# Attention on one Trainium2 core: the reciprocal of the softmax sums taken ahead of the first shift, and its transposes put between the third and fourth turn

## The chip, the core and the metric

The kernel runs on one core of a Trainium2 chip. The metric is the device time of one execution in microseconds (us). The kernel before takes 1241.21 us, the median of three runs from 1240.40 to 1241.44.

## The reference

The input x is one image of 128 x 128 positions with 64 channels. Four layers run one after the other, each as x = x + layer(group_norm(x)). The change touches the first one alone, attention along the rows of the image:

```
x = layernorm(pair)                                  # over 64 channels
q = (x @ Wq) * scale;  k = x @ Wk;  v = x @ Wv       # 4 heads of 32
bias = x @ Wb;  gate = sigmoid(x @ Wg + bg)
attn = softmax(q.k + bias, over the keys)            # per row i and head: 128 x 128
out = gate * (attn @ v)
x1 = pair + out @ Wo + bo
```

There are 128 rows, and in each row four heads of 128 x 128 scores, all in fp32. The other three layers are a windowed attention with a convolution, a graph diffusion in eight Runge-Kutta steps, and a row and column equivariant layer with 15 weights.

## The kernel before

Four rows make a group, so there are 32 groups (ROWS = 4, GROUPS = 32). The loop of the attention stage (`layer0_attention`, from L565) has 34 steps: in step g the engines work on three groups at once, as a pipeline. Group g is "own" (scores, shift, subtraction, exponential), group g - 1 is "past" (its probabilities are turned, weighted with v, and summed), and group g - 2 is "older" (its sums are inverted, and the result is gated, projected and added to x). Each engine has a list of its own, written out by hand in the order in which it runs, and waits at semaphores for the others; nothing reorders it.

The path of one group through the engines:

- TensorE makes the scores (`scores`, L789) in the PSUM banks called quad, one bank for each head.
- VectorE shifts them (`shift_head`, L703): for each of four rows of a head one instruction adds the bias, negates, writes the result to the SBUF tile `prob`, and keeps the least of each line in `least`. There are 16 for a group.
- GpSimd subtracts `least`, head by head (L639), and ScalarE takes the exponential in place, head by head (L667).
- One step later TensorE turns the probabilities (`turn`, L797), four transposes for each of four rows. The turned rows share two PSUM banks, so row 2 waits for ScalarE's copy (`keep_turn`, L662) of row 0, and row 3 for that of row 1. Then `weigh` (L803) makes attn @ v, and `add_up` (L811) the sums over keys, as products with a matrix that picks a head. VectorE copies the sums to SBUF (L759).
- One step later still, TensorE transposes the sums (L829, semaphore sums_turned) right behind its scores. VectorE takes their reciprocal (L722, rtotal_ready), 128 x 16 numbers. GpSimd spreads each of them over 32 columns (L645, rwide_ready). TensorE transposes that back, four transposes of 128 x 128 (L840, r_made), into the bank `total_bank`. VectorE multiplies it with 1 + tanh of the gate (L732) and with attn @ v (L738, gated_ready), TensorE projects with Wo (L852), and VectorE adds the result to x (L744, x1_ready).

TensorE's list in a steady step is thus: scores; transpose of the older sums; turns of rows 0 and 1; turns 2 and 3, each behind its copy; the four reciprocal transposes; q and k of the next group (L773, which waits until two heads of this group are shifted); gate and v of this group (L779, L782, which wait until all four copies of the turns are made, as they write to the same two banks); output projection (L852); weigh; add_up.

VectorE's list is: shift head 0; reciprocal; shift heads 1 and 2; factor and gated; shift head 3; x1; v with its bias (L751); copy of the sums; two statistics of x1 for the next layer (L762, L763). GpSimd's is: subtract head 0; spread; subtract heads 1 to 3; two copies of x1 to the other half of the partitions (L654). ScalarE's is: four copies of turns; exponential of head 0; q and k of the next group (L671, L673); exponential of head 1; tanh of the gate (L692); exponentials of heads 2 and 3.

The first two steps have no older group, the last two no own one, and the last one no past one. Step 31 has an own group, but no next one to project.

Of the kernel before, what the change touches and what calls it, by code (L numbers as in the profile page):

```python
# [16 lines left out]
HEADS, HD = 4, 32  # L17
ROWS = 4
# [546 lines left out]
def layer0_attention(nc, m, args):  # L565
# [19 lines left out]
    rtotal = m.take(ROWS * HEADS)  # L585
    rwide = m.take(CH)
# [4 lines left out]
    scores_made, shifted, lowered, exps_done = S("scores_made"), S("shifted"), S("lowered"), S("exps_done")  # L591
    turned, kept = S("turned"), S("kept")
    av_made, sums_made, sums_kept, sums_turned = S("av_made"), S("sums_made"), S("sums_kept"), S("sums_turned")
    rtotal_ready, rwide_ready, r_made, factor_ready, gated_ready = S("rtotal_ready"), S("rwide_ready"), S("r_made"), S("factor_ready"), S("gated_ready")
# [11 lines left out]
    def of_head(t, h):  # L606

        return t.rearrange("p (r h x) -> p h r x", r=ROWS, h=HEADS)[:, h, :, :]
# [11 lines left out]
    with nc.Block() as block:  # L620

        @block.sync
        def _(sp):
            sp.dma_start(wo, args["L0_conv_Wo"]).then_inc(wo_ready, 16)

        @block.gpsimd
        def _(pool):
            step = m.chain(pool, "pool")
            step(pool.memset(pick, 0.0))
            for h in range(HEADS):  # L630
                step(pool.memset(pick[:, h, h:h + 1], 1.0))
            pool.sem_inc(pick_ready, 1)  # L632
            for g in range(STEPS0):
                b = g % 2
                for h in range(HEADS):
                    if g < GROUPS:
                        pool.wait_ge(shifted, HEADS * g + h + 1)
                        scored = of_head(prob[b], h)
                        pool.tensor_tensor(scored, scored, of_head(least[b], h).broadcast_to([128, ROWS, L]),  # L639
                                           ALU.subtract).then_inc(lowered, 1)  # L640
                    if h == 0 and g >= 2:
                        pool.wait_ge(rtotal_ready, g - 1)
                        if g > 2:
                            pool.wait_ge(r_made, g - 2)
                        pool.tensor_copy(rwide.rearrange("p (x d) -> p x d", d=HD),  # L645
                                         rtotal.unsqueeze(2).broadcast_to([128, ROWS * HEADS, HD])).then_inc(rwide_ready, 1)
                if g >= 2:
                    pool.wait_ge(rwide_ready, g - 1)
                    if g < GROUPS:
                        pool.wait_ge(lowered, HEADS * (g + 1))  # L650
                    pool.wait_ge(x1_ready, g - 1)
                    for e in range(2):
                        there, here = slice(e * C, (e + 1) * C), slice((1 - e) * C, (2 - e) * C)
                        step(pool.tensor_copy(m.pairs(HALF * (g - 2), HALF, m.x1s)[there], m.pairs(HALF * (g - 2), HALF)[here]))  # L654
# [43 lines left out]
        @block.vector  # L698
        def _(dve):

            def shift_head(g, b, h):
                for r in range(ROWS):
                    last = dve.tensor_tensor_reduce(prob[b][:, at(r, h)], m.quad[:, h, row(r)], m.bias[:, row(h)],  # L703
                                                    -1.0, BIG, ALU.add, ALU.min, least[b][:, at(r, h, 1)])
                last.then_inc(shifted, 1)

            dve.wait_ge(wo_ready, 16)
            dve.tensor_scalar(wo, wo, 0.5, None, ALU.mult).then_inc(S("wo_halved"), 1)
            dve.wait_ge(m.sem("bias_laid"), 16 * 64)
            for g in range(STEPS0):  # L710
                b = g % 2
                own, past, older = g < GROUPS, 1 <= g <= GROUPS, g >= 2
                if own:
                    dve.wait_ge(scores_made, g + 1)
                    if g >= 2:
                        dve.wait_ge(turned, 4 * (g - 1))
                    shift_head(g, b, 0)
                if older:
                    dve.wait_ge(sums_turned, g - 1)
                    if g >= 3:  # L720
                        dve.wait_ge(rwide_ready, g - 2)
                    dve.reciprocal(rtotal.rearrange("p (r h) -> p r h", r=ROWS),  # L722
                                   total_bank[:, 0:128].rearrange("p (r x) -> p r x", r=ROWS)[:, :, 0:HEADS]).then_inc(rtotal_ready, 1)
                if own:
                    shift_head(g, b, 1)
                    shift_head(g, b, 2)
                if older:
                    dve.wait_ge(r_made, g - 1)
                    dve.wait_ge(th_ready, g - 1)
                    if g >= 3:  # L730
                        dve.wait_ge(gated_ready, g - 2)
                    dve.scalar_tensor_tensor(out=factor, in0=th[b], scalar=1.0, in1=total_bank[:, :],  # L732
                                             op0=ALU.add, op1=ALU.mult).then_inc(factor_ready, 1)
                    dve.wait_ge(factor_ready, g - 1)
                    dve.wait_ge(av_made, g - 1)
                    if g >= 3:
                        dve.wait_ge(out_made, g - 2)
                    dve.tensor_tensor(gated, av_bank[:, :], factor, ALU.mult).then_inc(gated_ready, 1)  # L738
                if own:
                    shift_head(g, b, 3)  # L740
                if older:
                    dve.wait_ge(out_made, g - 1)
                    inner = m.pairs(HALF * (g - 2), HALF)
                    dve.scalar_tensor_tensor(out=inner, in0=total_bank[:, 0:PAIR].rearrange("p (i c) -> p i c", i=2),  # L744
                                             scalar=m.bo[:, :], in1=inner, op0=ALU.add, op1=ALU.add).then_inc(x1_ready, 1)
                if own:
                    dve.wait_ge(th_ready, g + 1)
                    if g >= 2:
                        dve.wait_ge(av_made, g - 1)
                    for half, bank in enumerate((turn_a, turn_b)):  # L750
                        last = dve.tensor_tensor(v[b][:, half * 256:(half + 1) * 256].rearrange("p (i c) -> p i c", i=2),  # L751
                                                 bank[:, 256:512].rearrange("p (i c) -> p i c", i=2),
                                                 m.v_bias[:, :].unsqueeze(1).broadcast_to([128, 2, 128]), ALU.add)
                    last.then_inc(v_ready, 1)
                if past:
                    dve.wait_ge(sums_made, g)
                    if g >= 2:
                        dve.wait_ge(sums_turned, g - 1)
                    dve.tensor_copy(sums, total_bank[:, 0:128]).then_inc(sums_kept, 1)  # L759
                if older:  # L760
                    dve.wait_ge(x1_ready, g - 1)
                    dve.bn_stats(m.stats[:, (g - 2) * 6:(g - 1) * 6], inner)  # L762
                    dve.tensor_reduce(m.cell_parts[:, (g - 2) * KVW:(g - 1) * KVW],  # L763
                                      inner.rearrange("p r (k w) -> p k r w", k=KVW), AX.XY, ALU.add)

        @block.tensor
        def _(pe):
# [25 lines left out]
            def turn(g, r):  # L793
                for h in range(HEADS):
                    if r == 0:
                        pe.wait_ge(exps_done, HEADS * g + h + 1)
                    last = pe.transpose(m.bank[r % 2][:, row(h)], prob[g % 2][:, at(r, h)], ident)  # L797
                last.then_inc(turned, 1)
# [19 lines left out]
            for g in range(STEPS0):  # L818
                b = g % 2
                own, past, older = g < GROUPS, 1 <= g <= GROUPS, g >= 2  # L820
# [9 lines left out]
                if past:  # L830
                    pe.wait_ge(v_ready, g)
                    turn(g - 1, 0)
                    turn(g - 1, 1)
                    for r in range(2, ROWS):
                        pe.wait_ge(kept, 4 * (g - 1) + r - 1)
                        turn(g - 1, r)
                if older:
                    pe.wait_ge(rwide_ready, g - 1)
                    for r in range(ROWS):
                        last = pe.transpose(total_bank[:, row(r)], rwide[:, row(r)], ident)  # L840
                    last.then_inc(r_made, 1)
                if g + 1 < GROUPS:
                    pe.wait_ge(shifted, HEADS * g + 2)
                    project_qk(g + 1)
# [947 lines left out]
```

## Time and profile before

| what | value |
|---|---|
| median of 3 runs | 1241.21 us (1240.40 to 1241.44) |
| profiled execution | 1242.17 us, its span 1240.4 us |
| busy share of the span | PE 89%, PEld 62%, DVE 59%, ACT 46%, POOL 26% |
| mean granted TensorE clock | 0.939 of full speed |
| attention stage (L620 to L863) | about 156 to 459 us of the span |
| one steady step of it | 8.97 us |

PE is TensorE's matmul row and PEld its row of weight loads, which run ahead of the matmuls and beside them; every transpose here is a load and a matmul. DVE is VectorE, ACT ScalarE, POOL GpSimd. The span is the time from the first to the last instruction; the execution takes 1.8 us more than that. In a timeline row the first number is the start, the second the duration of the row's instructions together, the bracket at the end the idle time ahead of them on their engine and what ended it. The names after the operation are tiles: "quad", "bank" and "duo" are PSUM ("duo" holds total_bank and av_bank), "nat" holds `prob` and the turned rows, "arena" is the tile space in SBUF that holds q, k, v, rtotal, rwide and the rest.

### The profile page before, as it was taken

What the parts mean: (1) busy time and instruction counts of PE and PEld (TensorE: products, weight loads), DVE (VectorE), ACT (ScalarE), POOL (GpSimd) and SP (SyncE); (2) the same over time, 40 slices, a digit from 0 to 9 for tenths busy, and PEclk for the clock granted to TensorE, in tenths of its full rate; (3) what the DMA queues carried; (4) which work ended last, traced back from release to release, by engine and by line L of the source; (5) the groups of instructions that cost most, each with busy time, mean ns of one, the idle gap of its engine ahead of it and who ended that gap; (6) DMA issues with size and microseconds to landing.
All of it is one profiled execution on the core that took longest, in us unless ns stands there. A gap on an engine that the chain in (4) does not pass through costs nothing. (4 is left out here: it accounts for less than half of the span.)

```text
span 1240.4 us, 25484 instructions
## 1 busy us (share of the span) xinstructions
PE 1098.8 (89%) x9447; PEld 770.5 (62%) x9447; DVE 728.6 (59%) x3560; ACT 569.3 (46%) x1161; POOL 325.6 (26%) x466
## 2 busy tenths in 40 slices
PE   3677289999999969994999999999999999999688
PEld 2422067777777743443777677677777767776476
DVE  2521057787877752224566766766676677667235
ACT  1299556767676631002444444444444444443200
POOL 0100046656565631000112212221221122122111
PEclk9987679999999988995999999999999999999869
DMA  8000000000000000000000000000000000000002
GB/s 156 1 0 4 4 4 3 2 3 2 3 2 3 3 1 1 1 0 9 2 1 1 1 2 1 1 2 1 1 2 1 1 1 1 1 1 1 1 29 112
DMA packets 11487, 11.35 MB, mean 9 GB/s; under 512 B 4324, under 2 KB 9188, under 8 KB 11364
## 3 DMA queue, kind: packets, MB, share of 16 engines
q1 hardware_dynamic: 9266, 9.08, 2.9%
q8 instruction: 75, 1.23, 0.4%
q10 hardware_dynamic: 2098, 0.65, 0.3%
q14 instruction: 48, 0.39, 0.1%
HBM read 5.14 MB, written 4.23 MB: 8 GB/s over the span
## 5 line engine op out<-in xcount | busy, mean ns | idle before, releaser
L1460 PE MATMUL quad<-theta,nat 128*128 128x512 f32 x512 | 240.7, 593 | 0.0
L639 POOL TENSOR_TENSOR nat<-nat,arena 128x512 f32<-128x512 f32 x128 | 132.9, 1050 | 111.4 <-DVE arena L703 111.4
L1259 POOL TENSOR_TENSOR nat<-nat,const 128x512 f32<-128x512 f32 x32 | 40.6, 1268 | 439.4 <-DVE nat L1398 439.4
L1468 PEld LDWEIGHTS quad<-flat 128*128 128x128 f32 x768 | 104.6, 190 | 46.5 <-ACT flat L1290 25.1
L1468 PE MATMUL quad<-flat 128*128 128x128 f32 x768 | 123.8, 284 | 2.8 <-ACT flat L1290 1.7
L1460 PEld LDWEIGHTS quad<-theta,nat 128*128 128x128 f32 x512 | 87.5, 191 | 61.7 <-issue 61.7
L703 DVE CUSTOM_DVE_ANT_0 nat<-quad,arena 128x128 f32<-128x128 f32 x512 | 113.2, 283 | 9.7 <-PE quad L789 9.7
L1290 ACT ACTIVATE flat<-quad 128x256 f32<-128x256 f32 x192 | 73.4, 382 | 70.4 <-PE quad L1468 56.6
L662 ACT ACTIVATE nat<-bank 128x512 f32<-128x512 f32 x128 | 69.5, 595 | 57.2 <-PE bank L797 57.2
L1367 DVE SCALAR_TENSOR_TENSOR flat<-nat,c,duo 128x128 f32<-128x128 f32 x64 | 22.0, 345 | 102.0 <-PE duo L1477 102.0
L667 ACT ACTIVATE nat<-nat 128x512 f32<-128x512 f32 x128 | 77.2, 633 | 5.6 <-POOL nat L639 5.5
L797 PE MATMUL bank<-const,nat 128*128 128x128 f32 x512 | 70.0, 280 | 8.0 <-ACT nat L662 8.0
L1456 PE MATMUL bank<-nat 128*128 128x128 f32 x512 | 68.8, 278 | 0.3 <-DVE nat L1444 0.3
L797 PEld LDWEIGHTS bank<-const,nat 128*128 128x128 f32 x512 | 56.0, 141 | 18.1 <-ACT nat L662 15.6
L1456 PEld LDWEIGHTS bank<-nat 128*128 128x128 f32 x512 | 63.1, 194 | 0.9 <-DVE nat L1444 0.7
L1348 ACT ACTIVATE nat<-bank 128x512 f32<-128x512 f32 x32 | 19.1, 597 | 87.3 <-PE bank L1565 87.3
L1383 DVE MAX8 arena<-nat 128x8 f32<-128x128 f32 x128 | 27.9, 281 | 44.4 <-ACT nat L1327 44.4
L773 PE MATMUL quad<-flat,w 64*128 64x256 f32 x256 | 38.2, 419 | 15.0 <-POOLq L632 13.0
L1415 DVE CUSTOM_DVE_ANT_0 nat<-nat,duo 128x128 f32<-128x128 f32 x128 | 29.2, 284 | 37.1 <-PE duo L1576 37.1
L703 DVE DVE_READ_ACCUMULATOR2_ANT arena<- 128x1 f32 x512 | 42.6, 83 | 0.0
L671 ACT ACTIVATE arena<-quad,qkg_bias 128x512 f32<-128x512 f32 x32 | 22.0, 687 | 41.5 <-PE quad L773 41.5
L512 PE MATMUL quad<-arena,const 128*128 128x512 f32 x32 | 22.7, 798 | 20.5 <-ACT arena L475 20.5
(384 smaller groups left out, 2316.2 us busy)
## 6 DMA issues: line engine op xcount, KB each, us to landing
out<-nat SPq DMA_DIRECT2D x16, 256.0 KB, 2.0
arena<-flat SPq DMA_DIRECT2D x64, 4.0 KB
const<-in_constants ACTq DMA_DIRECT2D x1, 400.5 KB, 3.2
arena<-in_L_conv_Ws SPq DMA_DIRECT2D x1, 240.0 KB
flat<-arena SPq DMA_DIRECT2D x3, 32.0 KB, 4.3
nat<-in_x SPq DMA_DIRECT2D x4, 0.2 KB, 13.0
arena<-in_L_conv_Wq ACTq DMA_DIRECT2D x1, 32.0 KB, 7.8
arena<-in_L_conv_Wk ACTq DMA_DIRECT2D x1, 32.0 KB, 7.7
```

The costliest lines, as they stand in the source:

```text
L639: pool.tensor_tensor(scored, scored, of_head(least[b], h).broadcast_to([128, ROWS, L]), ALU.subtract).then_inc(lowered, 1)
L662: act.activation(pT[r], m.bank[r % 2][:, :], ACT.Copy).then_inc(kept, 1)
L667: act.activation(t, t, ACT.Exp, scale=-1.0).then_inc(exps_done, 1)
L703: last = dve.tensor_tensor_reduce(prob[b][:, at(r, h)], m.quad[:, h, row(r)], m.bias[:, row(h)], -1.0, BIG, ALU.add, ALU.min, least[b][:, ...
L773: last = pe.matmul(bank, m.w0[part, w * 128:(w + 1) * 128], m.z[part, cols], start=True, stop=True)
L797: last = pe.transpose(m.bank[r % 2][:, row(h)], prob[g % 2][:, at(r, h)], ident)
L1259: pool.tensor_tensor(quarters(rem), quarters(rem), ident.unsqueeze(1).broadcast_to([128, ROWS, 128]), ALU.add).then_inc(diag_added, 1)
L1290: act.activation(kept, m.quad[:, HALF * half:HALF * (half + 1), place * C:(place + 2) * C], ACT.Copy).then_inc(z_ready[half], 1)
L1415: last = dve.tensor_tensor_reduce(cor[:, col(n)], rem[:, col(n)], B[2][:, col(n)], 1.0, 0.0, ALU.add, ALU.add, deg[:, n:n + 1])
L1456: last = pe.matmul(B[0][:, col(n)], source[:, col(n)], source[:, col(n)], start=True, stop=True)
L1460: return pe.matmul(m.quad[:, n, :], vT[:, col(n)], m.theta[:, part, :], start=(part == 0), stop=False, skip_group_check=True)
L1468: last = pe.matmul(m.quad[:, row, place * C:(place + 2) * C], a8[g % 2][:, col(row)], zs[half][k % 2][:, n, :], start=False, stop=(k == 2) ...
```

## The change

On VectorE the reciprocal of the older sums goes ahead of head 0's shift, with its two waits. On GpSimd the spreading goes ahead of head 0's subtraction, with its waits. On TensorE the four reciprocal transposes go between the third turn (row 2) and the fourth (row 3), with their wait. No instruction is added or taken away, and each keeps its semaphores. In step 33 TensorE's list is as it was, and in steps 32 and 33 so are those of VectorE and GpSimd, which have no shift and no subtraction there.

```diff
@@ GpSimd
             for g in range(STEPS0):
                 b = g % 2
+                if g >= 2:
+                    pool.wait_ge(rtotal_ready, g - 1)
+                    if g > 2:
+                        pool.wait_ge(r_made, g - 2)
+                    pool.tensor_copy(rwide.rearrange("p (x d) -> p x d", d=HD),
+                                     rtotal.unsqueeze(2).broadcast_to([128, ROWS * HEADS, HD])).then_inc(rwide_ready, 1)
                 for h in range(HEADS):
                     if g < GROUPS:
                         ...
-                    if h == 0 and g >= 2:
-                        pool.wait_ge(rtotal_ready, g - 1)
-                        if g > 2:
-                            pool.wait_ge(r_made, g - 2)
-                        pool.tensor_copy(...).then_inc(rwide_ready, 1)
@@ VectorE
-                if own:
-                    dve.wait_ge(scores_made, g + 1)
-                    if g >= 2:
-                        dve.wait_ge(turned, 4 * (g - 1))
-                    shift_head(g, b, 0)
                 if older:
                     dve.wait_ge(sums_turned, g - 1)
                     if g >= 3:
                         dve.wait_ge(rwide_ready, g - 2)
                     dve.reciprocal(...).then_inc(rtotal_ready, 1)
+                if own:
+                    dve.wait_ge(scores_made, g + 1)
+                    if g >= 2:
+                        dve.wait_ge(turned, 4 * (g - 1))
+                    shift_head(g, b, 0)
                 if own:
                     shift_head(g, b, 1)
                     shift_head(g, b, 2)
@@ TensorE
                     turn(g - 1, 0)
                     turn(g - 1, 1)
-                    for r in range(2, ROWS):
-                        pe.wait_ge(kept, 4 * (g - 1) + r - 1)
-                        turn(g - 1, r)
+                    pe.wait_ge(kept, 4 * (g - 1) + 1)
+                    turn(g - 1, 2)
                 if older:
                     pe.wait_ge(rwide_ready, g - 1)
                     for r in range(ROWS):
                         last = pe.transpose(total_bank[:, row(r)], rwide[:, row(r)], ident)
                     last.then_inc(r_made, 1)
+                if past:
+                    pe.wait_ge(kept, 4 * (g - 1) + 2)
+                    turn(g - 1, 3)
```

## Rows read from the trace of the kernel before

**Rows 1.** Longest waits: engine, line, releaser; total us, times, longest us.

```profile
PEld duo L840 <- POOL arena L645: 16.7, 31, 1.4
...
PE duo L840 <- POOL arena L645: 9.5, 31, 1.2
...
PEld bank L797 <- ACT nat L662: 15.6, 32, 0.5
```

**Rows 2.** One stretch: us, busy us of five engines, PEclk, DMA share, GB/s.

```profile
200.00:300.00 100.00, 94.20 (x1569) 75.48 (x1565) 79.82 (x460) 69.82 (x135) 60.51 (x78) 1.00 0.01 2
```

**Rows 3.** Timeline, steady step, TensorE: start, duration, engine, line; idle before, releaser in brackets.

```profile
257.21 1.17 PE L789 MATMUL quad<-arena 32*128 32x128 f32 x32
...
258.32 0.33 PE L829 MATMUL duo<-const,arena 128*128 128x128 f32 x1
...
259.77 0.91 PEld L797 LDWEIGHTS bank<-const,nat 128*128 128x128 f32 x8 [0.49 <-ACT nat L662]
...
259.77 1.14 PE L797 MATMUL bank<-const,nat 128*128 128x128 f32 x8 [0.25 <-ACT nat L662]
...
261.19 0.42 PEld L840 LDWEIGHTS duo<-const,arena 128*128 128x128 f32 x4 [0.51 <-POOL arena L645]
...
261.19 0.66 PE L840 MATMUL duo<-const,arena 128*128 128x128 f32 x4 [0.28 <-POOL arena L645]
...
261.78 0.73 PEld L773 LDWEIGHTS quad<-flat,w 64*128 64x128 f32 x8 [0.17 <-issue]
...
262.53 0.41 PEld L779 LDWEIGHTS bank<-flat,w 64*128 64x128 f32 x4
...
263.72 0.20 PEld L852 LDWEIGHTS duo<-arena 128*64 128x64 f32 x4
...
268.74 0.91 PEld L797 LDWEIGHTS bank<-const,nat 128*128 128x128 f32 x8 [0.49 <-ACT nat L662]
```

**Rows 4.** Timeline, the same step, VectorE and GpSimd.

```profile
258.45 0.29 DVE L703 CUSTOM_DVE_ANT_0 nat<-quad,arena 128x128 f32<-128x128 f32 x1 [0.16 <-PE quad L789]
...
259.30 0.26 DVE L722 RECIPROCAL arena<-duo 128x16 f32<-128x16 f32 x1
...
259.47 0.23 DVE L703 CUSTOM_DVE_ANT_0 nat<-quad,arena 128x128 f32<-128x128 f32 x1
...
259.53 1.05 POOL L639 TENSOR_TENSOR nat<-nat,arena 128x512 f32<-128x512 f32 x1 [2.26 <-DVE arena L703]
...
260.53 0.61 POOL L645 COPY arena<-arena 128x512 f32<-128x512 f32 x1
...
261.89 0.69 DVE L732 SCALAR_TENSOR_TENSOR arena<-arena,duo 128x512 f32<-128x512 f32 x1 [0.70 <-PE duo L840]
...
262.61 0.69 DVE L738 TENSOR_TENSOR arena<-duo,arena 128x512 f32<-128x512 f32 x1
```

**Rows 5.** Timeline, the same step, ScalarE.

```profile
259.12 1.08 ACT L662 ACTIVATE nat<-bank 128x512 f32<-128x512 f32 x2 [1.58 <-PE bank L797]
...
260.46 1.09 ACT L662 ACTIVATE nat<-bank 128x512 f32<-128x512 f32 x2 [0.26 <-PE bank L797]
...
261.45 0.62 ACT L667 ACTIVATE nat<-nat 128x512 f32<-128x512 f32 x1
...
262.96 0.69 ACT L671 ACTIVATE arena<-quad,qkg_bias 128x512 f32<-128x512 f32 x1 [0.89 <-PE quad L773]
```

**Rows 6.** Timeline, step 1, TensorE weight loads.

```profile
171.64 0.91 PEld L797 LDWEIGHTS bank<-const,nat 128*128 128x128 f32 x8 [0.49 <-ACT nat L662]
...
172.71 0.73 PEld L773 LDWEIGHTS quad<-flat,w 64*128 64x128 f32 x8 [0.17 <-issue]
```

**Rows 7.** Timeline, end of the stage, TensorE: step 31's output product, then step 32.

```profile
442.79 0.20 PEld L852 LDWEIGHTS duo<-arena 128*64 128x64 f32 x4 [0.62 <-DVE arena L738]
...
447.19 0.91 PEld L797 LDWEIGHTS bank<-const,nat 128*128 128x128 f32 x8 [0.49 <-ACT nat L662]
...
448.06 0.47 PEld L840 LDWEIGHTS duo<-const,arena 128*128 128x128 f32 x4
```

More of the change, by code:

```diff
@@ L640, in _ @@
                                            ALU.subtract).then_inc(lowered, 1)
-                    if h == 0 and g >= 2:
-                        pool.wait_ge(rtotal_ready, g - 1)
-                        if g > 2:
-                            pool.wait_ge(r_made, g - 2)
-                        pool.tensor_copy(rwide.rearrange("p (x d) -> p x d", d=HD),
-                                         rtotal.unsqueeze(2).broadcast_to([128, ROWS * HEADS, HD])).then_inc(rwide_ready, 1)
                 if g >= 2:
```

## Prediction

> **What bounds the kernel now.** The list of waits comes first. In the attention stage TensorE waits for two things that come back every step: for ScalarE's copy of the first turn, and for the spread reciprocals that GpSimd makes. The second is seen 31 times, 16.7 us in all on the weight-load row [rows 1]; one of them is the last step's, up to 1.4 us, so the other thirty are 0.51 us each. On the matmul row the same waits sum to 9.5 us. The stretch by engine says who sets the pace: from 200 to 300 us TensorE's matmuls are busy 94.2%, VectorE 80%, ScalarE 70%, GpSimd 61%, at a granted clock of 1.00, the 2.4 GHz level [rows 2]. So this is a TensorE stage with two small holes in each step, and clock and DMA are no question in it.
>
> Then the timeline of one steady step (step 11). The reader should take T = 259.77, when the third turn starts; the next step's third turn starts at 268.74, so the period is 8.97 us [rows 3]. After T come eight turns' weight loads, 0.91 us; then the load row is idle 0.51 us until 261.19, when the reciprocal transposes start, and the projection of q and k starts at 261.78, T + 2.01. GpSimd's spreading runs from 260.53 to 261.14 [rows 4]: it ends just before the hole closes. It is late because it is queued behind the subtraction of head 0 (259.53, 1.05 us), and that behind the shifts of head 0. The other repeated hole, 0.49 us for the first copy just ahead of T, is not touched by the change.
>
> **TensorE's list.** It gets no instruction more or less; the four reciprocal transposes move between the third and the fourth turn, and the waits keep their number. What remains if the hole is gone? Step 32 shows it, since there GpSimd has no subtraction and the reciprocals are early: its third turn starts at 447.19, the reciprocal loads follow at 448.06, 0.87 us later and with no idle time, and take 0.47 us [rows 7]. With the 0.17 us that always stand ahead of the projection [rows 3] this makes T + 0.87 + 0.47 + 0.17 = T + 1.51. A second way agrees: step 1 has no reciprocal transposes at all and goes from the third turn to the projection in 172.71 - 171.64 = 1.07 us [rows 6]; four more loads at (0.91 - 0.14) / 7 = 0.11 us are 0.44, again T + 1.51. The gain is 2.01 - 1.51 = 0.50 us a step, if everything else keeps up.
>
> The unseen thing is the way back, from reciprocal transposes to the fourth turn. Both are transposes of 128x128 fp32. The nearest rows are the way there, which costs nothing [rows 7], and the 0.17 us ahead of the projection [rows 3]. A gain is excluded, as the loads already follow at their own spacing. I take 0 and keep 0.17 for the range.
>
> **Is the hole really filled?** The reciprocal now waits for the transpose of the sums, which ends at 258.65, instead of standing behind four shifts. VectorE follows TensorE by 0.07 us (scores end 258.38, shift starts 258.45), so the reciprocal runs 258.72 to 258.98. GpSimd starts its subtraction 0.23 us after the shifts of head 0 are issued [rows 4]; with all of that as its lag the spreading runs 259.21 to 259.82. The reciprocal transposes would want it at T + 0.44 = 260.21. It is there with 0.3 us or more to spare, so both ends of this cost are nothing. GpSimd is free for it, for it has been idle 2.26 us before its first subtraction.
>
> **What is pushed back on VectorE.** Behind the new wait stand all the shifts. The reciprocal takes 0.17 us of VectorE (259.30 to 259.47), so head 0's shifts start at 258.89 instead of 258.45, 0.44 late, and end at 259.74 (four take 0.85). Head 0's subtraction starts 0.44 late and ends at about 261.02; GpSimd has done the spreading already, so head 1's starts at 261.0 against 261.10 before. Heads 1 and 2 (eight shifts, 1.70) end at 261.44. Who waits for these? The projection of q and k wants two heads shifted, 260.6, against 261.28: 0.7 to spare. The exponential of head 0 stands behind ScalarE's fourth copy anyway (about 262.0, below): 0.9 to spare. The factor product wants the reciprocals on the other side of TensorE, now at T + 1.14 = 260.91, so it is VectorE's own list that ends last: it starts at 261.45 instead of 261.89 [rows 4], and the gated product ends at 262.86. The output product wants it at 263.72 - 0.50 = 263.22: 0.36 to spare. The later shift, subtraction and x1 steps go with these and come 0.44 earlier or more. I cost all of it at nothing.
>
> **What is pushed back on ScalarE.** This is the tight place. The fourth turn's loads now start at T + 0.88 instead of T + 0.44. ScalarE's copy of the third turn started 0.69 after T (260.46) [rows 5]; with 0.69 to 0.80 for the fourth it starts at T + 1.57 to 1.68, takes 0.55 to 0.60, and the projection of gate and v, which waits for it, may load from T + 2.2 to T + 2.3. It wants to at T + 1.51 + (262.53 - 261.78) = T + 2.26 [rows 3]. The cover is used up to within 0.05 us; the loads also run 0.2 us ahead of their products, which hides more. I take 0, and keep 0.05 for the range. The exponential of head 0 ends at T + 2.8, and ScalarE's next task, q and k, wants 262.96 - 0.50 = T + 2.69, starting 0.1 before the end of the one ahead as it does now: level.
>
> **The sum.** Steps 2 to 30 have the full pattern: 29 x 0.50 = 14.5 us. Step 31 has no next q and k to project, so the wait for the fourth copy is bare: its gate and v projection may load at T + 2.26, and its output product 1.19 us later [rows 3], at 439.2 + 3.45 = 442.65 instead of 442.79, where it stops for the gated product today [rows 7]: 0.1 us. Step 32 is a chain through VectorE, which starts when the reciprocals are turned, 0.44 us earlier: 0.4 us. Step 33 has no turns: 0. Together 15.0 us. The profiled execution took 1242.17 us (span 1240.4 and 1.8 around it), so 1227.2 by its own time; the median of the runs is 0.96 lower, 1241.21, and gives **1226.2 us**, down 1.2%.
>
> Matmul row and load row disagree on the hole: 0.28 us against 0.51 [rows 3]. I went by the loads, because the paths through steps 1 and 32 bear them out. The Trainium skill (TensorE: Matmul & The Clock Gate, section on what each phase is for) says that in a stream one matmul's drain lies under the next one's fill, which an isolated one cannot have; so a stop costs the refilling beside the idle time of the matmul row. By that rule a step gains more than 0.28, and the 0.50 from steps 1 and 32 agrees with it; without it the sum would be 29 x 0.28 + 0.5 = 8.6 us.
>
> **Rivals.**
> (a) *Only part comes, because the restart is not won back or a new small stop appears.* It is the gain of the matmul row, 0.28, or 0.50 less 0.17 for the way back, or a stop at gate and v for the fourth copy; 0.28 to 0.33 a step, 8.6 to 10 us: 1231 to 1233. For it: the zero cover on ScalarE. Against it: rows 6 and 7.
> (b) *The stop moves whole to the projection of gate and v.* If the fourth copy ended 0.5 us later than worked out, at T + 2.8, TensorE would stand there as long as it stood before: 1241. Against it: ScalarE is idle when the fourth turn is ready, and nothing is queued ahead.
> (c) *Slower: the shifts, held behind the sums.* If the chain shift, subtraction, exponential, next turn were what ends last, each of 30 steps would grow by the 0.44 us that it starts late: 13 us, 1254. It decides once its slack, 0.7 us at the q and k projection and 0.9 at head 0's exponential, is gone. For it: VectorE is busy 80% and everything else of the step is queued behind the new wait. Against it: both slacks, and GpSimd's idle time.
> (d) *More than forecast*, as the denser stream shortens the first copy's stop too: up to 0.1 us a step, 3 us, 1223. No row speaks for it.
>
> **Chances.** Forecast 0.72 (its own range 1224 to 1229); (a) 0.15, (b) 0.04, (c) 0.05, (d) 0.04. The range of 1223.5 to 1233 holds the forecast and most of (a). A measurement of this kernel can tell about 0.2%, 2.5 us, from no change: faster 0.91, same 0.04, slower 0.05.
>
> **What would show it.** In the changed kernel the wait of the reciprocal transposes for GpSimd is gone for steps 2 to 31 and stays only in step 33; the weight loads of the third turn, the reciprocals and the fourth turn stand in one row of about 1.3 us; the period is 8.47 us; the spreading starts before head 0's subtraction, near T - 0.6; the factor product has little or no idle time before it. The forecast is wrong if the period is above 8.7, if a wait of the gate and v projection for ScalarE's copy appears with more than 0.1 us a step, or if GpSimd or VectorE shows a longer stretch between its first subtraction and the last.

## The result, and the profile after

The changed kernel takes 1224.89 us, the median of four runs (1223.81 to 1226.11), against 1241.18 us for the kernel before, now the median of four: 16.3 us less, a ratio of 0.9868 with a 95% interval of 0.9852 to 0.9883. The forecast was 1226.2 us, with a range of 1223.5 to 1233. The span of the profiled execution fell from 1240.4 to 1224.3 us. Three single executions of the kernels below, one each of `vector_gpsimd`, `gpsimd_tensor` and `after_second`, ran at a mean granted clock of 0.31 to 0.65 and took 1616 to 3511 us, and every median and ratio here leaves them out.

The timeline of the weight loads in the same step, 11, to be read against [rows 3]:

```profile
254.94 0.42 PEld L797 LDWEIGHTS bank<-const,nat 128*128 128x128 f32 x4 [0.49 <-ACT nat L662]
...
255.33 0.47 PEld L839 LDWEIGHTS duo<-const,arena 128*128 128x128 f32 x4
...
255.77 0.47 PEld L797 LDWEIGHTS bank<-const,nat 128*128 128x128 f32 x4
...
256.40 0.73 PEld L773 LDWEIGHTS quad<-flat,w 64*128 64x128 f32 x8 [0.17 <-issue]
...
257.16 0.41 PEld L779 LDWEIGHTS bank<-flat,w 64*128 64x128 f32 x4
...
263.37 0.42 PEld L797 LDWEIGHTS bank<-const,nat 128*128 128x128 f32 x4 [0.49 <-ACT nat L662]
```

T, the start of the third turn's loads, is now 254.94. The third turn's four loads, the four reciprocal loads and the fourth turn's four follow 0.39 and 0.44 us behind each other, with no bracket, and the projection of q and k starts at 256.40, T + 1.46. It was T + 2.01, and T + 1.51 was forecast. The next T is 263.37, so the period is 8.42 to 8.43 us, where it was 8.97. From the projection to the next T everything is as long as it was: 6.96 us before (261.78 to 268.74), 6.97 now.

The other engines in that step, against [rows 4] and [rows 5]:

```profile
253.86 0.26 DVE L717 RECIPROCAL arena<-duo 128x16 f32<-128x16 f32 x1 [0.39 <-PE duo L829]
...
254.24 0.61 POOL L639 COPY arena<-arena 128x512 f32<-128x512 f32 x1 [1.79 <-issue]
...
256.51 0.60 ACT L662 ACTIVATE nat<-bank 128x512 f32<-128x512 f32 x1 [0.27 <-PE bank L797]
...
256.52 0.68 DVE L732 SCALAR_TENSOR_TENSOR arena<-arena,duo 128x512 f32<-128x512 f32 x1
```

The reciprocal is at T - 1.08, the spreading runs from T - 0.70 to T - 0.09 and ends 0.48 us ahead of the start of the transposes at T + 0.39. The factor product (256.52) has no idle time ahead of it: it waits in VectorE's list. ScalarE's fourth copy ends at 257.11, 0.05 us ahead of the gate and v loads at 257.16 in the first fence.

The list of waits over the stage:

```profile
PEld bank L797 <- ACT nat L662: 15.6, 32, 0.5
...
DVE arena L717 <- PE duo L829: 11.9, 30, 0.6
```

The wait of the reciprocal transposes for GpSimd, 16.7 us in [rows 1], is left only once, in step 33. The wait for the first copy is the same 15.6 us. What is new stands on VectorE: the reciprocal waits 30 times, 0.4 us each, for the transpose of the sums, and no wait of TensorE comes from it. In the stretch from 200 to 300 us the matmul row went from 94.2% to 97.0% busy, at the same granted clock of 1.00 [rows 2]:

```profile
200.00:300.00 100.00, 96.99 (x1684) 81.09 (x1684) 83.84 (x485) 74.64 (x143) 65.84 (x84) 1.00 0.01 3
```

The end of the stage, against [rows 7]:

```profile
423.41 0.42 PEld L797 LDWEIGHTS bank<-const,nat 128*128 128x128 f32 x4 [0.49 <-ACT nat L662]
...
425.63 0.30 PEld L779 LDWEIGHTS bank<-flat,w 64*128 64x128 f32 x4 [0.93 <-ACT nat L662]
...
426.70 0.20 PEld L854 LDWEIGHTS duo<-arena 128*64 128x64 f32 x4
...
431.11 0.42 PEld L797 LDWEIGHTS bank<-const,nat 128*128 128x128 f32 x4 [0.49 <-ACT nat L662]
...
433.70 0.20 PEld L854 LDWEIGHTS duo<-arena 128*64 128x64 f32 x4 [1.30 <-DVE arena L738]
```

In step 31 the wait for the fourth copy is bare, 0.93 us, as forecast; T to the output product is 3.29 us, where it was 3.58. In step 32 it is 2.59 us against 3.09. So the saving adds up: 15.84 us between the third turn of step 1 and that of step 31 (267.57 us before, 251.73 now), 0.28 between those of steps 31 and 32 (7.98 to 7.70), 0.50 in step 32. The first product of the next stage starts 4.50 us behind the start of the last output product, where it was 3.93, so 0.57 us are lost again and 16.05 are left; the spans differ by 16.1.

Half of the 0.57 us is the clock. These are the last output product before (first row) and now (second row):

```profile
456.94 0.84 PE L852 MATMUL duo<-arena 128*64 128x256 f32 x4 [1.50 <-DVE arena L738]
```

```profile
440.36 1.12 PE L854 MATMUL duo<-arena 128*64 128x256 f32 x4 [1.51 <-DVE arena L738]
```

TensorE waits more than it works in this last step, in both kernels alike, and then the granted clock falls from 1.00 to 0.50, the 1.2 GHz level. Before the change it fell while this product ran (mean 0.70 over its 0.84 us); now it fell just ahead of it (0.50 over its 1.12 us). In `tensor_only` and `after_second` it fell behind it, and the same product took 0.65 us at 1.00. The other 0.28 us stand between the product's end and the next stage's first product: 3.10 us before, 3.38 now. Here the clock is not the cause, since `vector_tensor` has 1.12 us for the product and 3.10 behind it, and `after_second` has 0.65 and 3.37. All kernels below that spread early have the longer value, save `spread_twice` with 3.09, and those that spread late have the shorter one; why is open.

### The profile page after: what moved, and what is told of

Read it like the earlier page. It is cut to its first block and busy times, and to the rows that moved or that the text cites. A ratio compares the mean times of both kernels' runs of the same rounds, so it can differ in the third digit from the quotient of the medians.

```text
span 1224.3 us, 25455 instructions
## 1 busy us (share of the span) xinstructions
PE 1089.6 (89%) x9447; PEld 771.5 (63%) x9447; DVE 726.5 (59%) x3560; ACT 571.1 (47%) x1161; POOL 326.3 (27%) x466
## 5 line engine op out<-in xcount | busy, mean ns | idle before, releaser
L1261 POOL TENSOR_TENSOR nat<-nat,const 128x512 f32<-128x512 f32 x32 | 40.6, 1268 | 440.5 <-DVE nat L1400 440.5
L662 ACT ACTIVATE nat<-bank 128x512 f32<-128x512 f32 x128 | 73.0, 597 | 66.0 <-PE bank L797 66.0
L797 PE MATMUL bank<-const,nat 128*128 128x128 f32 x512 | 73.5, 277 | 8.0 <-ACT nat L662 8.0
L797 PEld LDWEIGHTS bank<-const,nat 128*128 128x128 f32 x512 | 57.4, 141 | 15.9 <-ACT nat L662 15.6
L1350 ACT ACTIVATE nat<-bank 128x512 f32<-128x512 f32 x32 | 19.1, 597 | 87.4 <-PE bank L1567 87.4
L789 PE MATMUL quad<-arena 32*128 32x128 f32 x1024 | 39.4, 292 | 1.5 <-ACT arena L673 1.5
```

The costliest lines, as they stand in the source:

```text
L662: act.activation(pT[r], m.bank[r % 2][:, :], ACT.Copy).then_inc(kept, 1)
L789: last = pe.matmul(m.quad[:, h, row(r)], qT[b][head(h), row(r)], kT[b][head(h), row(r)], start=True, stop=True, tile_position=(h * HD, 0))
L1261: pool.tensor_tensor(quarters(rem), quarters(rem), ident.unsqueeze(1).broadcast_to([128, ROWS, 128]), ALU.add).then_inc(diag_added, 1)
```

## The experiments

The theory: in this stage TensorE's list sets the period, and a stop costs about its own length on the load row; another engine matters only by when it releases TensorE. The main rivals: the order of the transposes is what brings the gain; the later shifts and subtractions are on the path; the cover on ScalarE is gone. The three moves were taken alone and in pairs, in all combinations, and then three kinds of room were tested: the cover of the spreading, that of the fourth copy, and the hole for the first copy.

**1. Reciprocal and spreading early, TensorE's list as before** (`vector_gpsimd`): the diff of the change without its TensorE part.

> The reciprocal and the spreading are early, TensorE's list is the old one (reciprocal transposes behind the fourth turn). Theory (TensorE's list sets the period, a stop costs its own length): the old 0.51 us stop ahead of the reciprocal transposes is gone, the third turn to the projection of q and k takes 1.51 us against 2.01 before and 1.46 in the changed kernel; period 8.47, about 1226.3 us. The 0.05 left over is a stop of the fourth turn for the second copy. Rival (the place of the transposes is where most of the gain comes from): period 8.7 or more, 1233 us or more.

Measured: 1226.22 us, ratio 0.9877 (0.9859 to 0.9895). The load row:

```profile
255.42 0.91 PEld L797 LDWEIGHTS bank<-const,nat 128*128 128x128 f32 x8 [0.49 <-ACT nat L662]
...
256.30 0.47 PEld L840 LDWEIGHTS duo<-const,arena 128*128 128x128 f32 x4
...
256.93 0.73 PEld L773 LDWEIGHTS quad<-flat,w 64*128 64x128 f32 x8 [0.17 <-issue]
```

T to the projection is 1.51 us and the period 8.47, as worked out. So nearly all of the gain is here, and TensorE's move is worth 0.05 us a step. That 0.05 is a stop within the eight turns. Cut off at 255.92, the same row shows where the fifth load, the first of the fourth turn, begins, and below it are the copies of the first two turns:

```profile
255.42 0.63 PEld L797 LDWEIGHTS bank<-const,nat 128*128 128x128 f32 x5 [0.49 <-ACT nat L662]
```

```profile
254.77 1.09 ACT L662 ACTIVATE nat<-bank 128x512 f32<-128x512 f32 x2 [1.58 <-PE bank L797]
```

The copies end at 255.86 and the fifth load starts at 0.49 after T, 255.91, where the load that follows four others started 0.39 after T in the changed kernel. It had waited for the second copy: it starts 0.05 us behind the copy's end, as the third turn does behind the first copy's. The reciprocal transposes now stand in that hole.

**2. Only the spreading early** (`gpsimd_only`): the GpSimd part of the diff alone.

> Only the spreading goes ahead of head 0's subtraction; the reciprocal stays behind head 0's shift, TensorE's list is the old one. Theory: the reciprocal starts at T - 0.47 as before, the spreading 0.38 later, ready at T + 0.57, ahead of T + 0.87 where the transposes want it: no stop, period 8.47, 1226.3 us, as good as both moves. Rival (the reciprocal must be early): a stop remains, 1231 us or more. Second rival (the subtraction of head 0, 0.7 us later now, is on the path): 1241 us or more.

Measured: 1226.92 us, ratio 0.9886 (0.9870 to 0.9902), period 8.47. The step:

```profile
254.40 0.25 DVE L722 RECIPROCAL arena<-duo 128x16 f32<-128x16 f32 x1
...
254.78 0.61 POOL L639 COPY arena<-arena 128x512 f32<-128x512 f32 x1 [2.40 <-issue]
...
254.86 0.91 PEld L797 LDWEIGHTS bank<-const,nat 128*128 128x128 f32 x8 [0.49 <-ACT nat L662]
...
255.74 0.47 PEld L840 LDWEIGHTS duo<-const,arena 128*128 128x128 f32 x4
...
256.38 0.73 PEld L773 LDWEIGHTS quad<-flat,w 64*128 64x128 f32 x8 [0.17 <-DVE arena L703]
```

The spreading ends at 255.39, T + 0.53, ahead of the transposes at T + 0.88, with the reciprocal where it always was. Head 0's subtraction starts 0.7 us later than before the change, and nobody is late. One moved copy on GpSimd brings what the moves of reciprocal and spreading bring together.

**3. and 4. Only TensorE's move; only VectorE's move** (`tensor_only`, `vector_only`).

> Only the reciprocal transposes go between third and fourth turn; reciprocal and spreading come as late as before. Theory: TensorE stops at T + 0.39 until T + 1.42 and then still has the fourth turn to do, so the projection starts at T + 2.46 instead of T + 2.01: 0.45 a step, 13 us, about 1254 us. Rival (the stop only changes its place in the list): 1241 us.

> Only the reciprocal goes ahead of head 0's shift; the spreading stays behind head 0's subtraction, TensorE's list is the old one. Theory: shift and subtraction of head 0 start 0.44 us later and the spreading with them, so the transposes stop 0.95 us instead of 0.51: 13 us more, about 1254 us. Rival (an earlier reciprocal cannot hurt): 1241 us or less.

Measured: 1254.28 us, ratio 1.0105 (1.0087 to 1.0123), and 1252.19 us, ratio 1.0088 (1.0070 to 1.0107). The load rows, TensorE's move first:

```profile
264.31 0.42 PEld L797 LDWEIGHTS bank<-const,nat 128*128 128x128 f32 x4 [0.49 <-ACT nat L662]
...
265.73 0.42 PEld L839 LDWEIGHTS duo<-const,arena 128*128 128x128 f32 x4 [1.00 <-POOL arena L645]
...
266.76 0.73 PEld L773 LDWEIGHTS quad<-flat,w 64*128 64x128 f32 x8 [0.17 <-issue]
```

```profile
263.32 0.91 PEld L797 LDWEIGHTS bank<-const,nat 128*128 128x128 f32 x8 [0.49 <-ACT nat L662]
...
265.09 0.42 PEld L840 LDWEIGHTS duo<-const,arena 128*128 128x128 f32 x4 [0.86 <-POOL arena L645]
...
265.68 0.73 PEld L773 LDWEIGHTS quad<-flat,w 64*128 64x128 f32 x8 [0.17 <-issue]
```

Moved alone, the transposes stop 1.00 us where they stopped 0.51, and the projection is at T + 2.45; the period is 9.41. The early reciprocal alone makes the stop 0.86 us, where 0.95 was expected, and the period 9.32, where that makes 9.41: against T the spreading came 0.35 later, not 0.44. Two of the three moves are losses by themselves.

**5. and 6. VectorE's and TensorE's move; GpSimd's and TensorE's** (`vector_tensor`, `gpsimd_tensor`).

> Reciprocal early and transposes between third and fourth turn, but the spreading behind head 0's subtraction. Theory: the spreading is 0.44 us later than before (ready at T + 1.86) and the fourth turn stands behind it: projection at T + 2.9, 0.89 a step, 26 us, about 1268 us. Rival (costs do not add): 1254 us.

> Spreading early and transposes between third and fourth turn, the reciprocal behind head 0's shift. Theory: the spreading is ready at T + 0.57, the transposes want it at T + 0.39, so a stop of 0.18 us comes back: projection at T + 1.65, period 8.61, about 1230.5 us; here alone the early reciprocal is needed. Rival (the early reciprocal is worth nothing anywhere): 1225 us.

> The same kernel as the one with the spreading early and the transposes between third and fourth turn, the reciprocal behind head 0's shift, for a profile at the usual clock. Theory: the transposes stop about 0.15 us at T + 0.39, period 8.58, 1230 us. Rival (no stop): 8.42, 1225 us.

Measured: 1265.01 us, ratio 1.0186 (1.0168 to 1.0205), and 1229.0 us, ratio 0.9902 (0.9887 to 0.9917). The second kernel's rows come from its repeat, `gpsimd_tensor_again` (1228.81 us, one run). The load rows of both:

```profile
265.15 0.42 PEld L797 LDWEIGHTS bank<-const,nat 128*128 128x128 f32 x4 [0.49 <-ACT nat L662]
...
266.92 0.42 PEld L839 LDWEIGHTS duo<-const,arena 128*128 128x128 f32 x4 [1.35 <-POOL arena L645]
...
267.94 0.73 PEld L773 LDWEIGHTS quad<-flat,w 64*128 64x128 f32 x8 [0.17 <-issue]
```

```profile
263.71 0.42 PEld L797 LDWEIGHTS bank<-const,nat 128*128 128x128 f32 x4 [0.49 <-ACT nat L662]
...
264.28 0.42 PEld L839 LDWEIGHTS duo<-const,arena 128*128 128x128 f32 x4 [0.15 <-POOL arena L639]
...
265.31 0.73 PEld L773 LDWEIGHTS quad<-flat,w 64*128 64x128 f32 x8 [0.17 <-DVE arena L703]
```

In the first the stop is 1.35 us and the projection at T + 2.79 (2.9 expected), so the time is 3 us below the 1268 expected. In the second the transposes start at T + 0.57, to the hundredth where the spreading was expected, a stop of 0.15 us, and the projection is at T + 1.60 (1.65 expected). Only here, with the transposes moved, does the early reciprocal earn something: 1.60 against 1.46.

**7. How much cover has the spreading?** (`spread_twice`)

`step` runs an instruction and waits for its end; `spare` is a new tile, whose line is left out here.

```diff
...
+                    if g < GROUPS:
+                        step(pool.tensor_copy(m.spare.rearrange("p (x d) -> p x d", d=HD),
+                                              rtotal.unsqueeze(2).broadcast_to([128, ROWS * HEADS, HD])))
                     pool.tensor_copy(rwide.rearrange("p (x d) -> p x d", d=HD),
```

> The changed kernel, with a second copy of the same size ahead of the spreading on GpSimd, written to a spare tile and waited for: the spreading is ready 0.6 to 0.7 us later. Theory (0.44 us of cover ahead of the transposes): a stop of 0.2 to 0.3 us a step, 6 to 8 us more than the changed kernel, about 1232 us. Rival (no cover was left): 0.65 a step, 1244 us. Rival (more cover than that): 1225 us.

Measured: 1229.53 us, ratio 0.9903 (0.9888 to 0.9918), 4.6 us more than the changed kernel, where 6 to 8 were expected. The period is 8.62, 0.20 longer, which over 29 steps makes 5.8 us; the runs alone do not tell 4.6 from 5.8.

```profile
264.20 0.42 PEld L801 LDWEIGHTS bank<-const,nat 128*128 128x128 f32 x4 [0.49 <-ACT nat L666]
...
264.83 0.42 PEld L843 LDWEIGHTS duo<-const,arena 128*128 128x128 f32 x4 [0.21 <-POOL arena L643]
...
265.86 0.73 PEld L777 LDWEIGHTS quad<-flat,w 64*128 64x128 f32 x8 [0.17 <-DVE arena L707]
```

The transposes start at T + 0.63 instead of T + 0.39: 0.67 us more on GpSimd made them 0.24 late, so the cover is 0.43 us. The projection is only 0.20 late. The same 0.04 to 0.05 is missing in the second kernel of 5 and 6 (transposes 0.18 late, projection 0.14), in the kernel before (0.54 and 0.50), and in `vector_only` (0.89 and 0.85), `tensor_only` (1.03 and 0.99) and `vector_tensor` (1.38 and 1.33). The rows show where it goes: the four transposes' loads take 0.42 us behind a stop and 0.47 in the changed kernel, where they follow without one.

**8. and 9. Is the cover on ScalarE used up?** The copy of the fourth turn was made in two halves, and then in eight parts (`fourth_copy_halves`, `fourth_copy_eighths`). The edit shown is that for eight parts; for two halves the copy of r == 3 is written as two.

```diff
-                act.activation(pT[r], m.bank[r % 2][:, :], ACT.Copy).then_inc(kept, 1)
+                parts = 8 if r == 3 else 1
+                w = 512 // parts
+                for n in range(parts):
+                    last = act.activation(pT[r][:, n * w:(n + 1) * w], m.bank[r % 2][:, n * w:(n + 1) * w], ACT.Copy)
+                last.then_inc(kept, 1)
```

> The changed kernel, with ScalarE's copy of the fourth turn made in two halves, which takes 0.84 us instead of 0.60. In the changed kernel the copy ends 0.05 us ahead of the loads of the gate and v projection. Theory (the loads run 0.2 us ahead of the products, which hides a late copy): the loads stop 0.2 us, the products move by 0.03, at most 1 to 2 us more: 1226 us. Rival (cover really used up): 0.24 a step, 7 us, 1232 us.

> The changed kernel, with ScalarE's copy of the fourth turn made in eight parts of 64 columns. The two halves took 0.66 us where 0.84 was expected, so they tested a delay of 0.06 only. Eight parts should take about 1.0 us, the copy ends 0.4 late. Theory (the loads of the gate and v projection can start 0.2 us late before the products move): a stop of about 0.4 us on the load row, the projection's products 0.2 later than now: period 8.62, 6 us more than the changed kernel, 1231 us. Rival (no cover beyond the 0.06 seen): 0.4 a step, 12 us, 1237 us. Rival (cover of more than 0.4): 1225 us.

Measured: 1225.76 us, ratio 0.9869 (0.9856 to 0.9883), for two halves, which took 0.66 us together and made the gate and v loads 0.06 late and their products not at all (period 8.42). Eight parts took 1.04 us: 1235.24 us, ratio 0.9946 (0.9930 to 0.9963).

```profile
260.70 0.73 PEld L777 LDWEIGHTS quad<-flat,w 64*128 64x128 f32 x8 [0.17 <-issue]
...
260.81 1.04 ACT L665 ACTIVATE nat<-bank 128x64 f32<-128x64 f32 x8 [0.28 <-PE bank L801]
...
261.90 0.30 PEld L783 LDWEIGHTS bank<-flat,w 64*128 64x128 f32 x4 [0.47 <-ACT nat L665]
...
262.98 0.20 PEld L858 LDWEIGHTS duo<-arena 128*64 128x64 f32 x4
```

The gate and v loads start 1.20 us behind the projection's, where 0.76 is usual, so 0.44 late; the output product's start 2.28 behind it, where 1.94 is usual [rows 3], 0.34 late, and the period is 8.76. So 0.10 us of lateness is hidden, half of what this expectation counted on, and 10 us came instead of 6. It is made up on the load row itself: the gate's four loads take 0.30 us behind the stop and 0.41 without one.

**10. The other hole: the transposes between second and third turn** (`after_second`).

```diff
                     turn(g - 1, 1)
-                    pe.wait_ge(kept, 4 * (g - 1) + 1)
-                    turn(g - 1, 2)
                 if older:
                     pe.wait_ge(rwide_ready, g - 1)
...
                 if past:
+                    pe.wait_ge(kept, 4 * (g - 1) + 1)
+                    turn(g - 1, 2)
                     pe.wait_ge(kept, 4 * (g - 1) + 2)
```

> The changed kernel, with the reciprocal transposes between the second and the third turn, where TensorE stops 0.49 us for the first copy. Theory: the spreading is ready only 0.05 us ahead of the end of that stop, so the stop changes its owner and shrinks by 0.05: period 8.37, 1.5 us less, about 1223.5 us. Rival (the hole for the first copy is filled, and the stop is gone): 7.95 us a step, 1211 us. Rival (nothing changes): 1225 us.

Measured: 1223.4 us, ratio 0.9856 (0.9836 to 0.9876).

```profile
263.45 0.42 PEld L837 LDWEIGHTS duo<-const,arena 128*128 128x128 f32 x4 [0.44 <-POOL arena L639]
...
263.83 0.90 PEld L797 LDWEIGHTS bank<-const,nat 128*128 128x128 f32 x8
...
264.91 0.73 PEld L773 LDWEIGHTS quad<-flat,w 64*128 64x128 f32 x8 [0.17 <-issue]
```

The third turn no longer waits for the first copy; the transposes wait 0.44 us for the spreading instead, and the period is 8.37 to 8.38 (263.45 to 271.82). The stop has changed its owner and lost 0.05, as expected. By the runs alone the two kernels cannot be told apart; the periods differ.

**11. The sums transposed in the middle of the scores as well** (`sums_in_scores`). This is the kernel of 10 with one more move; the old place of the transpose, not shown, is kept for the last two steps.

```diff
-            def scores(b):
+            def scores(b, g=0):
                 for r in range(ROWS):
+                    if r == 2 and g >= 2:
+                        pe.wait_ge(sums_kept, g - 1)
+                        pe.transpose(total_bank[:, 0:128], sums, ident).then_inc(sums_turned, 1)
                     for h in range(HEADS):
```

> As the kernel with the transposes between second and third turn, and the transpose of the sums is taken in the middle of the scores (behind two rows of four), 0.5 us earlier in TensorE's list. Theory: reciprocal and spreading come about 0.4 us earlier, ready as the second turn ends, so the stop for the first copy is filled with the reciprocal transposes: 0.44 us a step less, minus 0.2 to 0.35 for the change of tile shape inside the scores; 3 to 7 us less than the changed kernel, 1218 to 1222 us. Rival (the break in the scores costs all of it): 1224 us or more. Rival (the break is free): 1212 us.

Measured: 1223.62 us, ratio 0.9863 (0.9845 to 0.9882). The gain of 3 to 7 us did not come; the rival in which the break in the scores costs all of it (1224 us or more) is the nearest.

```profile
267.93 0.54 PEld L792 LDWEIGHTS quad<-arena 32*128 32x128 f32 x16 [0.20 <-issue]
...
268.58 0.14 PEld L790 LDWEIGHTS duo<-const,arena 128*128 128x128 f32 x1
...
268.85 0.54 PEld L792 LDWEIGHTS quad<-arena 32*128 32x128 f32 x16
...
269.50 0.85 PEld L800 LDWEIGHTS bank<-const,nat 128*128 128x128 f32 x8
...
270.32 0.47 PEld L840 LDWEIGHTS duo<-const,arena 128*128 128x128 f32 x4
...
270.85 0.90 PEld L800 LDWEIGHTS bank<-const,nat 128*128 128x128 f32 x8
```

No row here has a bracket that names another engine, and the spreading is early enough. But two short waits for ScalarE are hidden in the last eight loads. Cut off at 271.34, that row shows its fifth load, the first of the fourth turn, and below it are the copies of the first two turns:

```profile
270.85 0.62 PEld L800 LDWEIGHTS bank<-const,nat 128*128 128x128 f32 x5
```

```profile
270.20 1.08 ACT L662 ACTIVATE nat<-bank 128x512 f32<-128x512 f32 x2 [1.94 <-PE bank L800]
```

The second copy ends at 271.28 and the fifth load starts at 271.33, 0.48 us behind the third turn's start where 0.39 is enough; the third turn in turn starts 0.53 us behind the reciprocal transposes, where 0.44 is enough. About half of each is made up in the loads that follow, as in experiment 7. From the first turn to the projection it is 2.42 us (269.50 to 271.92), where it is 2.85 in the changed kernel (253.55 to 256.40). Against this, from the first score to the first turn it is 1.57 us (267.93 to 269.50), where it is 1.16 in the changed kernel: two halves of the scores with the transpose between them cost 0.41 us more. The period is 8.39 to 8.40 (260.19 to 268.58 at the transpose of the sums), 0.02 to 0.03 less than in the changed kernel and no better than in 10. Filling the hole gained 0.43 us and cost 0.41.

## Why the prediction was right

*TensorE's list sets the period, and the hole is worth its length on the load row.* Right, and the bold choice of it, 0.50 a step and not 0.28, holds: `vector_gpsimd` gives 1.51 us from the third turn to the projection exactly as worked out from steps 32 and 1. With the kernel before and the delays of experiments 3 to 7 the rule is: what a late transpose costs is its lateness at the load row less 0.04 to 0.05. The sum by the matmul row, 8.6 us, is out. That refilling is what stands between the two rows, as the prediction argued, no run separates.

*The way back to the fourth turn costs 0.* The prediction kept between 0 and a loss of 0.17 for it and excluded a gain. That exclusion is the term that was mis-sized: the move gains 0.05 us a step, 1.5 us in all, since the fourth turn had been waiting for the second copy. The stop was inside a merged row of eight loads, which shows no bracket for it; that a run of eight took 0.91 us was read as its natural pace. Steps 1 and 32 have the same eight loads in one row of 0.91 us, so both ways to T + 1.51 had the stop in them and could agree without showing it. This is most of the 1.3 us by which the time came out below the forecast.

*The spreading is ready with 0.3 us or more to spare.* Right; it is 0.43. The lag from VectorE to GpSimd was taken as 0.23 us behind the reciprocal's end and is 0.12 (254.12 to 254.24); the reciprocal was taken at 0.33 + 0.07 behind the start of the transpose of the sums and came at 0.37. The transposes want it at T + 0.39, not T + 0.44, since the third turn's four loads stand behind a stop.

*What is pushed back on VectorE and GpSimd costs nothing.* Right. Rival (c), the slower one, is refuted by the changed kernel, whose first shift starts 0.41 us later against T (254.03) than before (258.45), and by `gpsimd_only`, in which head 0's subtraction is 0.7 us late and the period is still 8.47. The three kernels above 1250 us are slow by TensorE's stop, not by the shifts: their projection is later by as much as their period is longer (0.35 us in `vector_only`).

*ScalarE's fourth copy is level with the gate and v projection.* Right to within the reading: it ends 0.05 us before their loads. That the loads' lead of 0.2 us hides more was half right: 0.10 is hidden. Rival (b) had its mechanism, as the eighths show, and lacked its size.

*The sum.* Expected 29 x 0.50 + 0.1 + 0.4 = 15.0 us; the trace gives 15.84 for the steps to 31, which is 0.546 for each of 29, then 0.28, 0.50, and 0.57 lost at the start of the next stage. Step 31 was sized at 0.1 because its output product was put 1.19 us behind the gate and v loads; behind their stop it follows after 1.07 (425.63 to 426.70), and the loads came at T + 2.22 instead of T + 2.26. The 0.57 is a term that the sum does not have: it took everything behind step 33 as unchanged and the clock as no question, which holds for the loop and not for its last product. That the total missed by only 1.3 us is in part luck, for this loss stands against the three gains. Rivals (a) and (d) are out: no part of the 0.50 is missing, and the first copy's stop is as long as it was, 15.6 us.

## What to carry to other kernels

Where one in-order list sets the period, price a stop by comparing the same stretch in an iteration that lacks it (here the second and the last but one), not by the idle time of one row. Such a comparison inherits every stop that both iterations have, so cut merged rows open: a short wait inside a run of equal instructions has no bracket, as in experiments 1 and 11. Moves that feed each other must be priced together and one by one: here one moved instruction on GpSimd carries the gain, while each of the other two alone loses 11 to 13 us. When a hole is filled by reordering, look at what it costs to interrupt the stretch from which the filling is taken.

## What the runs showed of the hardware that was not expected

ScalarE's copies of 128 x 512 fp32 out of PSUM take 0.60 us each, those of 128 x 256 take 0.38, and those of 128 x 64 take 0.22 to 0.30. In a row they overlap: two of 256 columns take 0.66 us together (`fourth_copy_halves`) and eight of 64 take 1.04 (`fourth_copy_eighths`), each starting 0.10 to 0.12 us behind the one before. Behind a stop TensorE's load row makes up part of it: 0.05 us over four transposes of 128 rows (0.42 instead of 0.47 us), 0.10 over the gate's four loads of 64 rows (0.30 instead of 0.41). A 128-row transpose between products that use 32 rows of the array costs about 0.4 us more than one placed at the end of them (1.57 against 1.16 us), with no wait in the trace. The granted clock can fall on either side of one product in kernels that differ little: the last output product of this stage took 0.65, 0.76, 0.84, 0.90 or 1.12 us.
